# Four PSUM banks instead of two for the score matmuls of an attention loop

## The reference, cut to what matters

```python
x = x + attn_a(layernorm(x), w_qkv, w_proj)        # Nystrom attention, 64 landmarks
x = x + ffn(layernorm(x), weight, bias)            # 8-bit quantised linear layer
x = x + attn_b(layernorm(x), ...)                  # two transformer layers, below
x = x + ffn(layernorm(x), weight, bias)

# attn_b, each of its 2 layers, 16 heads of width 64, rotary factors on q and k:
q = q / math.sqrt(64)
probs = jax.nn.softmax(jnp.einsum('bqhd,bkhd->bhqk', q, k), axis=-1)
att = jnp.einsum('bhqk,bkhd->bqhd', probs, v)
x = x + att @ wo
x = x + gelu_like(_ln(x) @ w1 + b1) @ w2
```

## Time and profile before

| | |
|---|---|
| time before, median of 2 runs | 7495.78 us (7454.44 and 7537.13) |
| profiled execution, its time | 7444.05 us |
| its span, core 7 (the slowest) | 7442.5 us |
| instructions in the span | 59582 |

### The profile page before, as it was taken

The page is one execution under the profiler, slowest core; times in us unless marked ns, Lnnn a source line. Parts: engine busy times, 40 slices in busy tenths (PEclk is TensorE's granted clock), DMA queues, the critical chain, the costliest instruction groups (busy, mean ns, idle before and its releaser), DMA issues. The chain is left out here.

```text
span 7442.5 us, 59582 instructions; the slowest of 8 cores (7392.4 to 7442.5 us)
## 1 busy us (share of the span) xinstructions
PE 4907.9 (66%) x19784; PEld 2013.5 (27%) x19784; DVE 1421.0 (19%) x4016; ACT 2019.0 (27%) x3176; POOL 148.8 (2%) x145
## 2 busy tenths in 40 slices
PE   3766564257777777776687657777767776687823
PEld 1446331122122221222333322122212221333311
DVE  1122455321000110101211131010100101201154
ACT  2210110323433334332202213433343333211010
POOL 0000000000000000000000000000000000000000
PEclk9765566555555555555798855555555555787956
DMA  2200010100000000000253400000000000153511
GB/s 55 22 10 1 1 35 0 51 9 5 0 5 5 5 0 5 5 0 12 34 57 52 40 9 1 5 5 5 5 0 5 5 0 12 28 57 46 56 63 45
DMA packets 257123, 140.23 MB, mean 19 GB/s; under 512 B 210050, under 2 KB 243138, under 8 KB 256708
## 3 DMA queue, kind: packets, MB, share of 16 engines
q0 software_dynamic: 242928, 92.29, 10.8%
q1 hardware_dynamic: 13908, 44.13, 1.8%
HBM read 211.85 MB, written 16.78 MB: 31 GB/s over the span
## 5 line engine op out<-in xcount | busy, mean ns | idle before, releaser
L1323 ACT ACTIVATE cUT<-cps,cNEGC 128x512 bf16<-128x512 f32 x2048 | 1301.1, 686 | 1436.0 <-PE cps L1317 1433.5
L1317 PE MATMUL cps<-cQBUF,cKBUF 64*128 64x512 bf16 x2048 | 1120.5, 599 | 275.3 <-ACT cUT L1323 261.1
L1330 PE MATMUL cpsPV<-cUT,cVBUF 128*65 128x512 bf16 x2048 | 965.8, 625 | 481.6 <-ACT cUT L1323 481.6
L1355 DVE RECIPROCAL SMALL<-cps 128x1 f32<-128x1 f32 x512 | 83.9, 164 | 2956.9 <-PE cps L1349 2956.0
L1330 PEld LDWEIGHTS cpsPV<-cUT,cVBUF 128*65 128x65 bf16 x2048 | 277.3, 160 | 983.6 <-issue 983.6
L1317 PEld LDWEIGHTS cps<-cQBUF,cKBUF 64*128 64x128 bf16 x2048 | 166.8, 102 | 1357.7 <-issue 1357.7
L1513 PE MATMUL dpsH<-XNFM,WBUF 128*128 128x512 bf16 x2048 | 470.0, 395 | 49.8 <-DMA WBUF<-bw 48.9
L1349 PE MATMUL cps<-IDF,cSOFT 65*128 65x65 f32 x512 | 171.9, 342 | 182.0 <-DVE BIG L1357 87.0
L1513 PEld LDWEIGHTS dpsH<-XNFM,WBUF 128*128 128x128 bf16 x2048 | 206.3, 101 | 313.1 <-issue 126.8
L1560 PE MATMUL dpsH<-BIG,WBUF 128*128 128x512 bf16 x1024 | 241.9, 391 | 47.5 <-DMA WBUF<-bw 47.5
L1257 PE MATMUL cps<-WBUF,XNFM 128*128 128x128 bf16 x2048 | 223.6, 276 | 46.6 <-DVE cKBUF L1239 46.6
(11 more groups left out here) (297 smaller groups left out, 4205.9 us busy)
## 6 DMA issues: line engine op xcount, KB each, us to landing
WBUF<-bw POOLq DMA_DIRECT2D x64, 1024.0 KB, 10.1
X<-x SPq DMA_DIRECT2D x1, 8192.0 KB, 29.9
spill<-X SPq DMA_DIRECT2D x1, 8192.0 KB, 30.2
XTMPF<-spill SPq DMA_DIRECT2D x16, 512.0 KB, 4.1
y<-X SPq DMA_DIRECT2D x1, 8192.0 KB, 22.0
WBUF<-wqkv POOLq DMA_DIRECT2D x24, 256.0 KB, 6.8
pbFP32S<-fw SPq DMA_DIRECT2D x8, 512.0 KB, 3.5
WBUF<-bwq POOLq DMA_DIRECT2D x16, 256.0 KB, 4.6
```

The source lines that it names most:

```text
L1317: t.matmul(pse2[:, :], KBUF[r0:r0 + 64, kb * 128:(kb + 1) * 128], QBUF[r0:r0 + 64, qg * 512:(qg + 1) * 512], start=True, stop=True), inc="ts")
L1323: s.activation(out=uts[:, qg * 512:(qg + 1) * 512], in_=pse2[:, :], func=AF.Exp, bias=NEGC[:, hh:hh + 1]), inc="ss")
L1330: last = t.matmul(psPV[0:65, qg * 512:(qg + 1) * 512], VBUF[:, hh * 1040 + kb * 65: hh * 1040 + (kb + 1) * 65], uts[:, qg * 512:(qg + 1) * ...
L1355: v.reciprocal(out=SM[:, mc:mc + 1], in_=psn[:, 64:65])
```

## The change

Score m uses one of four banks (`ps2`, `ps3`, `ps0`, `ps1`) by m modulo 4, and waits for exponential m-4 instead of m-2. Because `ps0` and `ps1` are also the banks of the transposes L1349, the first four scores of every head but the first of a layer also wait for the last normalisation of the head before.

```diff
                             for qg in range(4):
                                 m = kb * 4 + qg
-                                pse2 = ps2 if m % 2 == 0 else ps3
+                                pse2 = [ps2, ps3, ps0, ps1][m % 4]
                                 w2 = [("ss", s_c)] if m == 0 else []
-                                if m >= 2:
-                                    w2.append(("ss", e_ev[m - 2]))
+                                if m < 4 and h > 0:
+                                    w2.append(("vs", v_norm[h * NTT - 1]))
+                                if m >= 4:
+                                    w2.append(("ss", e_ev[m - 4]))
```

## The result

| | before | after |
|---|---|---|
| time, median | 7461.17 us (10 runs) | 7278.61 us (11 runs) |
| ratio of after to before | | 0.976, 95% interval 0.9722 to 0.9798 |
| profiled execution's span, slowest core | 7442.5 us | 7266.5 us |

The forecast was 7275 us and a ratio of 0.977.

The account below looks back on a forecast made before the run. Bound: a closed TensorE-ScalarE chain of 5.44 us per key block, 512 times, neither engine full. From a base of 7449, minus 179 for four banks, plus 5 for extra waits: 7275 us; range 7195 to 7365.

Parts of the forecast that it names:

- The chain: Attention loop: each key block is one closed TensorE-ScalarE chain of 5.44 us, falling to 5.09, 512 x 0.35 = 179 us gained.
- Slower: Rival 5: projections between head pairs lose their full clock, 370 us more, giving 7645 us; chance 0.03.
- Its two parts: The gain per key block: ScalarE's idle 0.25 us plus 0.10 to 0.11 of lost overlap between exponentials, taken as 0.35.
- Rival 2: Attention loop: only the idle gap goes, later exponentials don't overlap; 128 us gained, 7321 us; chance 0.10.
- The waits: Loop profile: scores' waits for exponentials gone, ScalarE's near 1305 us, V matmuls' about 1.38 each (700 us), L1303 to L1317 unchanged.
- The new wait on VectorE: First scores of a head wait for the previous head's last normalisation: already satisfied, 5 us counted for the waiting instructions.
- the cover that the prediction named: Before a head's score 0: two VectorE reductions stand behind the normalisation, so the new wait is met 2.2 us early.
- No contention: Exponentials reading one bank while TensorE writes others more densely: no slowing, priced at nothing; 0.09 each would eat the gain.
- The clock: TensorE's clock in the loop stays at 0.50 despite 3.4 us without a break, since operands fill half the array.
- Rival 1: TensorE's clock rises in the loop, counted for half the blocks: 269 us less, giving 7006 us; chance 0.13.
- No gain: Rival 4: something else paces the exponentials and the third starts where it does today; 7449 us; chance 0.03.
- The larger wait of ScalarE: Each key block: ScalarE's wait of 2.67 us stays, because no score moves ahead of the V matmuls.

Follow-up runs that it names:

- e2: Kernel before with its two banks, plus only the new wait of a head's first scores on the last normalisation: 7452.38 us, ratio 0.9997.
- e3: Changed kernel with score matmuls contracting 128 rows, Q kept twice with 64 rows zero: 6895.88 us, ratio 0.9253 to the kernel before.
- e4: Changed kernel with the next block's scores put ahead of this block's V matmuls on TensorE: 6571.9 us, ratio 0.8727 to the kernel before.
- e7: Changed kernel with V matmuls of 128 stationary columns instead of 65, extra sums unread: 7293.79 us, ratio 0.975 to the kernel before.
- e9: Kernel before, two banks and old waits kept, with 128-row scores (half of Q zero): 7126.29 us, ratio 0.945.
- e6: Kernel before, two banks kept, with the next block's scores ahead of this block's V matmuls: 7038.66 us, ratio 0.935.
- e5: Changed kernel with scores ahead of the V matmuls and 128-row scores together: 5935.86 us, ratio 0.7945 to the kernel before.

## Why the prediction was right

- **The chain.** The prediction drew a closed chain, 0.70 + exponentials + 0.14 + 1.81, with everything but the exponentials unchanged. After: 0.70 to the first exponential (2399.45 to 2400.15), 2.42 of exponentials (forecast 2.43), 0.15 to the V matmuls and 1.82 of these: 5.09, as forecast. The gain in this block was 0.35 for 0.35. That 512 x 0.35 = 179 us stands so near the 7442.5 - 7266.5 = 176 us between the two spans is in part luck. The loops of the 32 heads went from 2797.5 to 2609.8 us (the profiled core of each kernel), 187.7 less or 0.37 per block: the 0.36 that the prediction had read from its rows and turned down was the nearer number, and a few blocks before were longer than the one shown. Outside the loops 12 us came back, most of it in the projections (see "Slower").
- **Its two parts.** The idle 0.25 and the lost overlap of 0.10 both came: four exponentials in one row of 2.42 are three steps of 0.58 and one of 0.69. Rival 2 (only the idle time) would have left about 2.5.
- **The waits.** Forecast: L1319's waits for exponentials gone (they are), ScalarE's near 1305 us (1310.8), the one before L1332 about 1.38 us each and 700 in total (1.39, 712.9). One small point was wrong: L1303 to the first score is not unchanged, it is 0.11 longer, for the price of a wait that is already met (e2).
- **The new wait on VectorE** costs nothing beyond that, some 3 us in all where the prediction counted 5, by e2 and with the cover that the prediction named.
- **No contention.** The exponentials last 687 ns in the median after and 688 before.
- **The clock.** The forecast of no rise in the loop held, and half of its reason did: the operands' size, but of the two operands that it named only the 64 rows of the scores matter, not the 65 columns of V. That had been the weakest step, with one row for it (L718) and one against (L1033, a run as long). e3, e4, e7 and e9 now show it: all matmuls of the loop with 128 rows, the clock rises; scores with 64 rows, it stays at 0.50 even with TensorE never idle; columns filled, nothing. It isn't the average of the rows either, an estimate from these traces says: e4's block has 96 rows at work on average without a break and stays at 0.50, while e9's at that clock would have 128 rows for 8 x 0.43 of 5.44 us, 81 on average, and rises. What it is about a 64-row matmul that keeps the clock down is left open, and scores with 128 rows of real data instead of zeros weren't tried. Rival 1, with its chance of 0.13, would have come true with 128-row scores. Its price was also near: a full-clock block is 3.90 us, and the working gave 4.04.
- **No gain** did not happen. The result that the prediction cited beside it, from the Trainium skill, "TensorE: Matmul & The Clock Gate", section "HAM oscillation — how this bites in real kernels" (PSUM double-buffering gave no further gain in one kernel), does not carry over: the trace does not agree here, since the bank was a link of the chain.
- **Slower** did not happen, but a little of it did. In the 14 stretches between one pair of heads and the next (the projections, and the end and start of a head), the mean clock was 0.70 before and 0.68 after, averaged over the eight cores, and they took 14 us longer in all, on average over the cores and on the two profiled ones (724.8 and 739.2 us). That is the deal of the clock that the prediction had allowed +-50 us for, and it hid that the loops gained 9 us more than forecast.
- **What it missed** was not in the sum but beside it. The larger wait of ScalarE, 2.67 us a block, was named and left as given. The experiments show what it takes to shorten it: four banks give 0.35 us a block in the old order of work; scores ahead with two banks give 0.97 (e6), and four banks add 0.81 to that, 1.78 together (5.44 - 3.66).

## What to carry to other kernels

When two engines hand work to each other and neither is full, write down one turn of the loop as a closed chain with its rows; a change is worth what it takes off that chain, times the turns. Here that was within 5% of what the loops gained (179 for 188 us); that the whole time came out to 0.1% is luck. A bank more is worth only as much as the order of work lets it run ahead: look whether the next turn's first step can be put before this turn's last one. And read the granted clock beside the operand shapes: this loop, which sat at the lower level with half the rows in use in every second group, was lifted by filling them, with zeros.

## What the runs showed of the hardware that I had not expected

- In these runs the granted clock of TensorE depends on the rows that its matmuls use, and not only on whether it is busy. 64-row scores: 0.50 with 40.00 of 40.00 us busy (e4). 128-row scores with half of Q zero: 0.83 in a window of the loop with 33.48 of 60 us busy (e3), and 1.00 with the scores ahead (e5). 128 stationary columns instead of 65: 0.50 (e7). The Trainium skill, "TensorE: Matmul & The Clock Gate", section "What's actually happening", says that the gate follows how busy TensorE has been; e4's 0.50 does not agree with that if busy means only that matmuls run.
- A semaphore wait that is already met costs 0.11 us where it stands on the path (e2: 16.5 against 13.3 us over the 32 heads, 30 of which have it).
- From one group of four 512-column matmuls to the next, where the operands and the bank group change, TensorE loses 0.09 to 0.13 us at 1.2 GHz (1.81 and 1.85 against 4 x 0.43), in e4 where nothing waits.
- The weight load of 128 columns took less time than that of 65: 128 against 170 ns in the median, at the same clock of 0.50 (e7 and the changed kernel).
